# One attention kernel, its matrix units in a new order: fewer changes of the array's shape in a round, two of them side by side that stood apart, more unused products at the start

## What is computed

```python
xn = _layernorm(x, axis=-1)
q, k, v = (_split_heads(xn @ W) for W in (Wq, Wk, Wv))
w = softmax(einsum('bhqd,bhkd->bhqk', q, k) / DH + causal) * mask
w = w / (sum(w) + 1e-08)
attn = einsum('bhqk,bhkd->bhqd', w, v) -> (B, S, H*DH) @ Wo
x_int = clip(round(xn / scale), -127, 127); ffn = (x_int * scale) @ (ternary - 1).T + bias
return x + attn + ffn
```

## Time and profile before

| | us |
|---|---|
| median of 3 runs | 1005.23 (1003.13 to 1008.03) |
| the profiled execution's own time | 1006.92 |
| its span, first to last instruction | 1005.2 |
| PE busy | 988.9 (98%) |
| DVE, POOL, ACT busy | 757.1 (75%), 706.2 (70%), 451.5 (45%) |
| granted TensorE clock, mean | 0.990 |

### The profile page before, as it was taken

One profiled execution on the slowest core, in us unless ns is written; L12 is line 12 of the kernel. 1 busy time (PEld: TensorE's weight loads), 2 busy tenths in 40 slices (PEclk: granted clock), 3 DMA queues, 4 the chain that ended last, 5 costly groups with the idle time before them and its releaser, 6 DMA issues.

```text
span 1005.2 us, 19181 instructions
## 1 busy us (share of the span) xinstructions
PE 988.9 (98%) x7107; PEld 635.0 (63%) x7107; DVE 757.1 (75%) x1706; ACT 451.5 (45%) x607; POOL 706.2 (70%) x649
## 2 busy tenths in 40 slices
PE   8999999999999999999999999999999999999997
PEld 3656666666666666666666666666666666666664
DVE  6778888778788778877767877677876677777754
ACT  4244444444444444554444444444453444454442
POOL 8567677668776668777767677668776667677672
PEclk8799999999999999999999999999999999999999
DMA  6000000000000000000000000000000000000000
GB/s 175 3 2 2 1 2 2 3 2 3 1 23 2 3 2 2 1 3 2 3 12 12 2 3 2 2 2 2 2 2 15 11 3 2 2 2 2 2 2 22
DMA packets 16133, 8.52 MB, mean 8 GB/s; under 512 B 5404, under 2 KB 15644, under 8 KB 16040
## 3 DMA queue, kind: packets, MB, share of 16 engines
q1 hardware_dynamic: 15416, 7.15, 2.7%
q10 hardware_dynamic: 624, 0.14, 0.1%
HBM read 4.33 MB, written 2.10 MB: 6 GB/s over the span
## 4 chain that ended last, share of the span: by engine, by line
PE 91%; DVE 5%; issue 1%; POOL 1%; DMA 1%; ACT 1%; SPq 0%; DVEq 0%; ACTq 0%; POOLq 0%
PE ring L1006 26%; PE pv L1023 25%; PE ring L968 12%; PE beside L1065 7%; PE beside L1038 6%; PE ring L941 3%; PE ring L937 3%; PE ring L938 3%; PE ring L955 2%; DVE ring L768 1%; PE ring L956 1%; PE ring L957 1%; DVE v L755 1%; PE beside L1053 1%; PE pv L1071 1%
## 5 line engine op out<-in xcount | busy, mean ns | idle before, releaser
L567 ACT ACTIVATE prob<-ring 128x1024 f32<-128x1024 f32 (+3 forms) x384 | 293.6, 810 | 349.6 <-PE ring L1006 349.5
L501 POOL TENSOR_TENSOR psumd<-psumd,prob 128x512 f32<-128x512 f32 (+1 forms) x250 | 406.0, 1624 | 28.9 <-POOL psumd L501 1.3
L768 DVE CUSTOM_DVE_ANT_0 ring<-ring,causal 128x128 f32<-128x128 f32 (+3 forms) x512 | 240.2, 517 | 97.6 <-PE ring L968 97.0
L1006 PE MATMUL ring<-q,k 64*128 64x512 f32 (+3 forms) x2304 | 281.3, 349 | 1.8 <-DMA mrow<-maxrow 0.8
L1023 PE MATMUL pv<-prob,v 128*64 128x512 f32 (+3 forms) x1536 | 267.1, 490 | 0.0
L474 POOL TENSOR_SCALAR_AFFINE_SELECT prob<-prob 128x256 f32<-128x256 f32 x256 | 109.4, 429 | 216.4 <-ACT prob L567 214.3
L1006 PEld LDWEIGHTS ring<-q,k 64*128 64x128 f32 x2304 | 195.7, 186 | 37.7 <-DVE rowmax L768 5.3
L1023 PEld LDWEIGHTS pv<-prob,v 128*64 128x64 f32 x1536 | 104.9, 137 | 154.1 <-issue 141.5
L772 DVE TENSOR_REDUCE rowmax<-ring 128x2 f32<-128x1024 f32 x128 | 151.5, 1222 | 6.2 <-PE ring L968 2.7
L497 POOL TENSOR_TENSOR psumd<-prob 128x768 f32<-128x768 f32 (+1 forms) x63 | 132.5, 2103 | 25.5 <-ACT prob L567 20.5
L968 PE MATMUL ring<-k,q 64*128 64x512 f32 (+3 forms) x768 | 145.4, 415 | 5.1 <-DVE k L744 1.5
(11 more groups left out here) (120 smaller groups left out, 943.8 us busy)
## 6 DMA issues: line engine op xcount, KB each, us to landing
kext<-kext SPq DMA_DIRECT2D x128, 4.0 KB, 1.7
out<-x_sb SPq DMA_DIRECT2D x8, 256.0 KB, 2.5
x_sb<-in_L_attn_query SPq DMA_DIRECT2D x3, 512.0 KB, 5.5
mrow<-maxrow SPq DMA_DIRECT2D x62, 4.0 KB
x_sb<-in_L_attn_query SPq DMA_DIRECT2D x2, 256.0 KB, 4.3
xn_sb<-in_L_attn_Wv SPq DMA_DIRECT2D x1, 512.0 KB, 5.4
wo<-in_L_attn_Wo SPq DMA_DIRECT2D x1, 512.0 KB, 7.0
xn_sb<-in_L_attn_Wq SPq DMA_DIRECT2D x1, 448.0 KB, 3.5
```

Of the source, the lines that this page charges most:

```text
L501: g.tensor_tensor(acc[:, :, lo:HALF], acc[:, :, lo:HALF], pr[:, :, lo:HALF], ALU.add).then_inc(acc_done, 1)
L567: a.activation(prob[n % NPROB][:, :, lo:HALF], ring[:, slot(f"S{t}", i), :, lo:HALF], ACT.Exp, scale=1.0 / DH).then_inc(exp_done, 1)
L768: last = v.tensor_tensor_reduce(out=ring[:, s, h, 0:n], in0=ring[:, s, h, 0:n], in1=causal[:, HALF - n:HALF], scale=1.0, scalar=MASKED, op ...
L1006: last = t_.matmul(ring[:, s, h, lo:HALF], k[p][rows, keys], q[p][rows, cols], start=(at == 0), stop=(at == len(parts) - 1))
```

## The change

Six things are changed. In each round D1 of the pair before stands right behind its G11; S0 to S4 follow one another; Y0 of the pair before, V and Y1 of the pair before stand together. So PE goes through 8 changes between the three shapes in a round, where it went through 14. From G3 on, M and S alternate without Y0 between them. X0 and X1 become one unit X that takes a slot of the ring; its full-precision copy is made by POOL (xf), which adds the two parts. On DVE and ACT the names are set in an order to match, and the quantisation step moves behind o1. At the front, eight unused products replace six (the two new ones are 256 wide), and four more I units stand among the first maxima, two of them between K and M0 of pair 0, two in the later half.

```diff
-PE_PLAN = ("T Q+ K+ X0 X1 W G11- M0+ M1+ S0 S1 S2 M2+ D1- M3+ S3 V+ S4 S5 M4+ S6 M5+ Y1- M6+ M7+ S7 D0 G3 "
-           "M8+ S8 S9 S10 M9+ Y0 M10+ M11+ S11 G7")
-ACT_PLAN = "Z Qhi+ Khi+ X0 X1 E0 E1 E2 ln1- ex1- E3 E4 E5 E6 E7 ln0 ex0 E8 E9 E10 E11"
-DVE_PLAN = ("Tc Z Qlo+ Klo+ R0+ R1+ X0 X1 W R2+ R3+ t1- u1- Vs+ o1- R4+ R5+ Ya1- R6+ R7+ t0 u0 R8+ o0 q "
-            "R9+ R10+ Ya0 R11+")
+PE_PLAN = ("T Q+ K+ G11- D1- M0+ M1+ S0 S1 S2 S3 S4 M2+ M3+ Y0- V+ X Y1- M4+ S5 S6 M5+ W S7 M6+ D0 G3 "
+           "M7+ S8 M8+ S9 M9+ S10 S11 M10+ M11+ G7")
+ACT_PLAN = "Z Qhi+ Khi+ ln1- ex1- E0 E1 E2 E3 E4 X E5 E6 E7 ln0 ex0 E8 E9 E10 E11"
+DVE_PLAN = ("Tc Z Qlo+ Klo+ R0+ R1+ t1- u1- o1- q R2+ Ya0- R3+ Vs+ X R4+ Ya1- W R5+ R6+ t0 u0 R7+ o0 R8+ "
+            "R9+ R10+ R11+")
...
-PE_FIRST = ("Q+ K+ M0+ M1+ M2+ I0+ M3+ I1+ M4+ I2+ M5+ I3+ H+ M6+ I4+ M7+ I5+ M8+ M9+ M10+ M11+ "
-            "S0+ S1+ T+ S2+ S3+ Q++ K++ V+")
+PE_FIRST = ("Q+ K+ I0+ I1+ M0+ M1+ M2+ I2+ M3+ I3+ M4+ I4+ M5+ I5+ H+ M6+ I6+ M7+ I7+ M8+ I8+ M9+ I9+ M10+ I10+ "
+            "M11+ S0+ S1+ T+ S2+ S3+ Q++ K++ V+")
...
-        NIDLE = 6
+        NIDLE = 8
...
+            def rows_of_parts(b):
+
+                pool.wait_ge(x2_done, 2 * b + 2)
+                pool.wait_ge(fq_step, (b - 1) * FQ_STEPS + 1)
+                g.tensor_tensor(xf[:, :], x1[b % 2][:, :].bitcast(F32), x2[b % 2][:, :].bitcast(F32), ALU.add
+                                ).then_inc(xf_done, 2)
```

More of the change, by code:

```diff
@@ L47 @@
 ACT_FIRST = "xf0+ Qhi+ xf1+ Khi+ keys+ rest+ Hrow+ wv+ E0+ E1+ E2+ E3+ Qhi++ Khi++"
-PE_LAST = "T G11- S0 S1 S2 D1- S3 S4 S5 S6 Y1- S7 D0 G3 S8 S9 S10 S11 Y0 D1 F1 G7 G11 Y1"
+PE_LAST = "T G11- D1- S0 S1 S2 S3 S4 Y0- S5 Y1- S6 S7 D0 G3 S8 S9 S10 S11 Y0 D1 F1 G7 G11 Y1"
 POOL_LAST = "L0 A0 L1 A1 L2 A2 L3 A3 L8 L9 L10 L11"
-DVE_LAST = "Tc t1- u1- o1- A5 Ya1- A6 A7 t0 u0 o0 A8 A9 Ya0 t1 u1 o1 Ya1"
+DVE_LAST = "Tc t1- u1- o1- q Ya0- A5 Ya1- A6 A7 t0 u0 o0 A8 A9 Ya0 t1 u1 o1 Ya1"
 SP_PLAN = "mrow kext+ store-"
@@ L69, in happens @@
 def happens(name, i):
-    if name in ("X0", "X1"):
-        return i % PAIRS_OF_BATCH == 4 + int(name[1:]) and i < N_PAIRS - PAIRS_OF_BATCH
+    if name in ("X", "xf"):
+        return i % PAIRS_OF_BATCH == (4 if name == "X" else 5) and i < N_PAIRS - PAIRS_OF_BATCH
     if name == "W":
@@ L79, in happens @@
     if name == "q":
-        return i % PAIRS_OF_BATCH < PAIRS_OF_BATCH - 1
+        return i % PAIRS_OF_BATCH > 0
     if name == "Z":
@@ L105 @@
 PE_ORDER = list(walk(PE_PLAN, PE_FIRST, PE_LAST))
-IN_RING = [("X", -2)] + [u for u in PE_ORDER if u[0][0] in "QKSMV" or u == ("D1", LAST)]
-IN_BESIDE = [u for u in PE_ORDER if u[0][0] in "THDYXWF" and u not in (("D1", LAST), ("Y1", LAST))]
+IN_RING = [("X", -2)] + [u for u in PE_ORDER if u[0][0] in "QKSMVX" or u == ("D1", LAST)]
+IN_BESIDE = [u for u in PE_ORDER if u[0][0] in "THDYWF" and u not in (("D1", LAST), ("Y1", LAST))]
 PLACE = {u: n for n, u in enumerate(IN_RING)}
@@ L508, in _ @@
                     add(i, int(name[1:]))
+                elif name == "xf":
+                    rows_of_parts(batch_of_turn(i - 1))
                 else:
@@ L541, in turned_high, with turned_whole @@
                 a.activation(x1[b % 2][:, c * HALF:(c + 1) * HALF], src, ACT.Copy).then_inc(x1_done, 1)
[L543 to L548, removed]
+            def turned_whole(c, src):
+                act.wait_ge(x2_done, c + 1)
                 a.activation(xf[:, c * HALF:(c + 1) * HALF], src, ACT.Copy).then_inc(xf_done, 1)
@@ L604, in _ @@
                     inverses(i, int(name[2:]))
-                elif name[0] == "X":
-                    turned_high(batch_of_turn(i), int(name[1:]), beside[:, :])
-                    turned_whole(batch_of_turn(i), int(name[1:]), beside[:, :])
+                elif name == "X":
+                    for c in range(2):
+                        turned_high(batch_of_turn(i), c, ring[:, slot("X", i), c, :])
                 elif name[:2] == "xf":
-                    turned_whole(0, int(name[2:]), ring[:, slot("X", -2), int(name[2:]), :])
+                    turned_whole(int(name[2:]), ring[:, slot("X", -2), int(name[2:]), :])
                 elif name == "rest":
@@ L865, in _ @@
                 elif name == "q":
-                    quantise(i // NPB, i % NPB + 1)
-                elif name[0] == "X":
-                    turned(batch_of_turn(i), int(name[1:]), beside[:, :])
+                    quantise(i // NPB, i % NPB)
+                elif name == "X":
+                    for c in range(2):
+                        turned(batch_of_turn(i), c, ring[:, slot("X", i), c, :])
                 elif name == "Z":
@@ L894, in slot_left @@
                     pe.wait_ge(v_done, j + 1)
+                elif j < 0:
+                    pe.wait_ge(xf_done, 2)
                 else:
-                    pe.wait_ge(xf_done, 2)
+                    pe.wait_ge(x2_done, 2 * batch_of_turn(j) + 2)
             def beside_left(name, i):
@@ L911, in beside_left @@
                     pe.wait_ge(y_added, halves_upto(j, int(unit[1:])))
-                elif unit[0] == "X":
-                    pe.wait_ge(x2_done, 2 * batch_of_turn(j) + int(unit[1:]) + 1)
                 else:
@@ L1074, in _ @@
             for n in range(NIDLE):
-                idle_products(HALF)
+                idle_products(HALF if n < NIDLE - 2 else 2 * P)
             for c in range(2):
@@ L1105, in _ @@
                     output_projection(i, int(name[1:]))
-                elif name[0] == "X":
-                    turn(batch_of_turn(i), int(name[1:]), beside[:, :])
+                elif name == "X":
+                    for c in range(2):
+                        turn(batch_of_turn(i), c, ring[:, slot("X", i), c, :])
                 else:
```

4 lines of the change are left out of this document (2 added, 2 removed).

## The result

The changed kernel takes 1008.78 us in the median (1007.77 to 1014.31, 12 runs) beside 1006.78 us for the kernel before on the same chip (1002.87 to 1008.03, 12 runs). The ratio is 1.0037, with an interval of 1.0023 to 1.0052: 2 to 5 us slower; the two medians are 2.0 us apart. 1009.5 was predicted. The profiled execution took 1008.93 us and its span is 1007.2.

The account below looks back on a forecast made before the run. PE, busy 988.9 of 1005.2 us, was taken to set the end. Steady part +11.7 (10.2 - 2 + 2 + 1.5) and front -5.5 gave +6, 1011 against the median, lowered to 1009.5 us; range 999 to 1017.

Parts of the forecast that it names:

- Changes of shape: PE's switches between matmul shapes: 14 a round become 8, each costing 0.20 us, counted as 1.15 us a round saved.
- S9 behind R7: S9 takes M7's slot and waits until DVE's R7 releases it: 0.72 us a round.
- The rule of the prediction: A unit with a late slot loses release time minus PE's end of the unit ahead, plus 0.165 us.
- E8: ACT's exponential of S8, for which M9 waited in the kernel before: 0.21 us lost, counted as gone.
- E1: ACT's exponential that frees S1's slot for S4; waits of S1 to S4 together 0.53 us a round.
- The pace: Ordinary round: new waits 2.23, less 0.75 old waits and 1.15 shape changes, +0.33 us; +10.2 over 31 rounds.
- The normalising rounds: Twelve rounds where DVE normalises other batches: D1 between K and S0 gives Qlo and Klo time, 2 us gained.
- X in the ring: Three rounds where S6 takes X's slot and waits for copies and subtractions: about 0.7 us each, +2.
- The last round: Without Q and K the runs of S stand closer and D1 waits for A11: +1.5 us, an estimate.
- The front: Start of the kernel: clock held for most of the maxima, -5 us, and -1.5 in part for 45 to 50; together -5.5.
- the waits are the smaller part: Rival, chance 0.17: S9 to S11 wait below 0.9 us together, round 1.0 us shorter, 980 to 990 us.
- the clock falls at the front: Rival, chance 0.28: PE's clock falls at the start as before, +1.5 instead of -5.5, about 1015.5 us.

Follow-up runs that it names:

- the kernel with the short R7: Changed kernel with R7 reducing only the first 128 of the 512 columns of each half; 999.91 us, 0.9964 of the kernel before.
- the front alone: Kernel before with only the changed front, its rounds as they were; 1002.30 us (0.9982), run again for a profile 1000.58 us (0.9935).
- the ten-change order: Changed kernel reordered from V on, M5 to M9 around D0 and G3, S8 to S11 in a row, ten shape changes; 999.70 us, 0.9926 of the kernel before.
- the last two orders: Changed kernel with S7 moved behind M7, 1001.94 us (0.9983 of the kernel before), and the ten-change order, 999.70 us (0.9926).

## Why the prediction was right, point by point

**Direction and size.** 1009.5 was predicted and 1008.78 measured. That they are 0.7 us apart is in part luck: I forecast 4.3 us above a median of 1005.2 from three runs, and the twelve runs beside the changed kernel put the median of before at 1006.78, 2.0 below it. The sum before I lowered it, +6 on the profile's span, was 4 us too high. Its steps, each against what was measured:

*Changes of shape, 0.20 each, six fewer.* Measured at 0.18 by two changes added. The saving is 1.1 instead of 1.15 us a round. This was right. The Trainium skill, TensorEngine Tiling (Array Packing), Key Properties, says that changing the tiling mode drains TensorE; the trace agrees, with 0.18 us for one, and a kernel that has six fewer is slower all the same.

*S9 behind R7.* 0.72 forecast. S9 starts 0.64 late (from 842.22, where M8's columns end, to 842.86; that M8 takes 0.05 is seen in the kernel with the short R7, where S9 follows it at 803.77), and it loses 0.11 more inside, 0.81 to M9 where its stream is 0.70: 0.75 in all. The rule of the prediction gives 842.80 - 842.22 + 0.165 = 0.745, so it holds for the whole loss, with the end of R7's record as the release. It also holds for M9 in the kernel with the short R7: E8's record ends at 804.94, S9's columns at 804.52, and the rule's 0.58 is 0.48 ahead of M9 and 0.10 inside it. The start itself follows the release by 0.05 or 0.06; the rest is lost in the first matmuls. I had counted 0.72, 0.31 and 0.27 at S9, S10 and S11, 1.30 in all. From the end of M8's columns to M10 it is 3.01 us, of which 0.70 + 0.12 + 0.47 + 0.39 = 1.68 are the streams of S9, M9, S10 and S11 as I had them: 1.33 lost. S4 starts at 828.88, late behind E1 as forecast, and S7 at 836.38, 0.37 behind M5, which has 0.23 us of columns; both lose about 0.1 more inside, where the first three pairs of S4 take 0.80 and those of S7 0.81 for 0.69 in S8. From S0 to M2 it is 3.95 us for streams of 3.38, so 0.57 for the forecast 0.53, and S7 loses 0.25 for 0.26. Summed over PE's units, the time beyond the columns' pace is about 4.0 us in an ordinary round and was about 3.7.

*The pace.* +0.33 forecast, +0.27 measured. The mechanism is right and the size close; over the 30 rounds behind round 0 it is 8.1 us for 9.9.

*The normalising rounds, -2.* Rounds 1 to 11 took 1.1 us more than before in all; 11 rounds at 0.27 would be 3.0. So -1.9, which is a remainder and agrees with the forecast. Half of it is round 2, 1.07 us above an ordinary round before and none after: there S0 had waited 0.75 us for k, at 102.29. In one round the forecast cover failed: in round 12 DVE is busy with the normalisation until 397.82, Qlo and Klo follow, and S0 waits 0.58 us for k. That costs 0.8, once.

*X in the ring, +2.* **This term was wrong.** In the round of the last X, PE's timeline has S5's last pair and S6, the unit that takes X's slot:

```profile
652.91 0.39 PE L1013 MATMUL ring<-mrow,kext 64*128 64x512 f32 x2
653.13 0.93 PE L1013 MATMUL ring<-q,k 64*128 64x512 f32 x6
```

S6 starts 0.22 later, when the columns of the pair are through. DVE's two subtractions start at 651.78 and end at 653.06, just in time; S6's first three pairs take 0.77 for 0.69. So Y1, M4 and S5 cover it all but 0.1, not all but 0.7. The rounds of X and the one behind it take 61.03 us (30.95 and 30.08) for 60.62 (30.20 and 30.42), +0.41, less than 2 x 0.27.

*The last round, +1.5.* +0.9 measured, from the last T to the end.

*The front, -5.5.* The first T comes 4.6 us earlier, where I had -5 for 15 to 35 us. The clock stayed up through the maxima, the case that I thought the likelier. Round 0 is 1.6 shorter, where I had -1.5 in part for the dip of 45 to 50 and +0.3 for the pace. **That step was wrong in its mechanism**: the dip is as long as before. What it costs is seen in the profiles without it. With the old rounds, round 0 takes 28.95 us in the front alone (no dip) and 30.45 in the kernel before; with the new rounds it takes 27.93 in the kernel with the old front (no dip behind 35 us) and 28.83 in the changed kernel. So the dip costs 1.5 us where it falls on a PE busy for 5.00 of 5 us, and 0.9 where it begins while PE is busy for 3.40 and DVE for 4.95. The rest, 1.0 us (27.93 for 28.95), goes with the new order, which is shorter in round 0 and not longer. The kernels that are compared here differ in their fronts too, so these three figures are near and not exact.

The sum closes: 6.2, less 2 for X, 1.8 for the pace, 0.6 for the last round and 1.0 for the front with round 0 (-6.2 for -5.2), plus 0.8 for round 12 and 0.3 for round 30 (30.36 us), is +1.9, and the spans differ by 2.0.

**The rivals.** That the waits are the smaller part is refuted: S9 to S11 lose 1.33 together, and the bound that I had set was 0.9. That the clock falls at the front is refuted by its 1.00. The even trade is close to what the median shows, though not by its mechanism: the round does lose 0.27, and the front returns most of it. I lowered the sum from 1011 to 1009.5 with a doubt on waits in series. Nothing bears that reason out: the waits came as summed, and the sum was too high for X, the pace, the last round and the front. The lowered figure was nearer by luck. D1 did not wait for POOL; the only wait of a D for POOL, 1.5 us, is that of D0 in the last round, which I had not forecast.

**Where the six changes' worth went.** 6 x 0.18 = 1.1 us a round were saved, and 0.27 more than that was lost again in the ring. Taking away the R7 delay gives 0.25, putting S7 behind M7 0.26, moving M7 ahead of D0 nothing. No single wait carries the loss, since behind each stands another: R7, then E8 at M9, then R9 at M10. What I can't settle is why the ten-change order stops at 29.53 to 29.87 with the forecast at 29.5, and whether an order with eight changes and none of these waits exists. It wasn't tried.

## What to carry to other kernels

On an engine that shows 98% busy, count what a round costs from start to start and not by busy time: what a unit spends beyond its columns is the change of shape (0.18 us) and the slot that came late, and a plan that removes one can buy the other. A ring of three slots makes the order of the producers an order for the consumers too; before moving a unit, write down for the unit three places on when its slot is released, and carry the delay along to the next two units, because removing the largest wait (0.75 with what it costs inside) gave back only 0.25. And compare a kernel with the runs of before at the same granted clock, or the gain of the front comes out as anything from 1 to 6 us.

## What the runs showed of the hardware

Full-array units of two kinds, V and Y1, follow each other without any loss of the kind that a change of shape costs: V's matmuls in the changed kernel start every 0.12 us from the second on, and Y1 follows the last of them at the same distance. Between Y0 and V there is a small loss, 0.20 us from V's first matmul to its second (831.32 to 831.52), for a reason that no run here shows.

```profile
832.70 0.28 PE L964 MATMUL ring<-wv,x 128*128 128x256 f32 x1
832.82 1.06 PE L1072 MATMUL beside<-wo,o 128*128 128x128 f32 x8
```

I had not expected that the kernel before would have two clusters of times, 1002.3 to 1004.4 and 1005.1 to 1008.2 us, with the mean granted clock as the only difference that the records show (0.995 or 0.996, and 0.988 to 0.993). The changed front does not remove this: with it, single runs of four of the kernels fell to 0.990 and took 4 to 7 us more than the rest (1009.03 for the front alone, 1014.31 for the changed kernel, 1004.03 and twice near 1007 for the last two orders). What decides which an execution gets, no run here shows.
